# A four-layer transformer kernel: the second layer's feed-forward adapts its weights on VectorE alone, with its even rows spread by a transfer

## The reference, cut to what matters

```python
def _layernorm(x, axis=-1, eps=1e-05):
    m = jnp.mean(x, axis=axis, keepdims=True)
    v = jnp.var(x, axis=axis, keepdims=True)
    return (x - m) / jnp.sqrt(v + eps)

def _L1_ffn_ref(x, W1, b1, W2, b2, scale):          # x: (4, 512, 256), W1: (1024, 256), W2: (256, 1024)
    lt = x[:, 1:17, :]                              # 16 rows of each batch
    even, odd = lt[:, ::2, :], lt[:, 1::2, :]       # 8 rows each
    m1 = (even[:, :4, :, None] * odd[:, :4, None, :]).reshape(4, 1024, 256)
    m2 = (even[:, 4:, :, None] * odd[:, 4:, None, :]).reshape(4, 256, 1024)
    h = einsum('bsd,hd->bsh', x, W1) + scale * einsum('bsd,bhd->bsh', x, m1) + b1
    h = gelu(h)
    return einsum('bsh,oh->bso', h, W2) + scale * einsum('bsh,boh->bso', h, m2) + b2

x = x + _L1_ffn_ref(_layernorm(x), ...)
x = x + _L2_xattn_ref(_layernorm(x), ctx, ...)      # which begins with another layer norm (ln1), times g, plus b
```

## Time and profile before

| | us |
|---|---|
| median of 3 runs | 3356.65 |
| lowest, highest | 3354.74, 3372.45 |
| the profiled execution's own time | 3362.91 |
| its span in the profile | 3361.1 |
| TensorE busy | 2767.6 (82%) |
| VectorE busy | 1979.2 (59%) |
| ScalarE busy | 1440.4 (43%) |
| GpSimd busy | 1143.6 (34%) |
| mean granted clock of TensorE | 0.893 |
| the feed-forward's stage | 941.9 to 1126.3 |

### The profile page before, as it was taken

The page is one execution under the profiler, slowest core; times in us unless marked ns, Lnnn a source line. Parts: engine busy times, 40 slices in busy tenths (PEclk is TensorE's granted clock), DMA queues, the critical chain, the costliest instruction groups (busy, mean ns, idle before and its releaser), DMA issues. The chain is left out here.

```text
span 3361.1 us, 45805 instructions
## 1 busy us (share of the span) xinstructions
PE 2767.6 (82%) x17268; PEld 1590.7 (47%) x17268; DVE 1979.2 (59%) x3643; ACT 1440.4 (43%) x1932; POOL 1143.6 (34%) x1030
## 2 busy tenths in 40 slices
PE   5888887778879899998877898788999998698544
PEld 3343343633336444445743444377777777233122
DVE  4655666577547454445757556664454443677688
ACT  2556556247522254455224455423333432366422
POOL 3233232213133246565325777540010110222333
PEclk7999988889879999999988999889999999699766
DMA  7556651156310001112000000001211121564100
GB/s 170 115 117 142 120 130 34 38 112 136 72 48 1 16 33 40 43 48 72 26 13 1 1 1 1 26 1 37 98 56 43 65 66 51 111 114 105 36 10 15
DMA packets 129740, 198.58 MB, mean 59 GB/s; under 512 B 36272, under 2 KB 66480, under 8 KB 129392
## 3 DMA queue, kind: packets, MB, share of 16 engines
q1 hardware_dynamic: 97776, 143.23, 18.9%
q0 software_dynamic: 31744, 52.41, 5.5%
HBM read 130.73 MB, written 64.75 MB: 58 GB/s over the span
## 5 line engine op out<-in xcount | busy, mean ns | idle before, releaser
L2293 DVE TENSOR_REDUCE L_mx<-bank_t 128x2 f32<-128x1024 f32 (+3 forms) x512 | 565.1, 1121 | 335.0 <-PE bank_t L2104 215.3
L2293 DVE TENSOR_REDUCE L2a_mx<-bank_t 128x2 f32<-128x1024 f32 x256 | 311.4, 1223 | 366.9 <-PE bank_t L2081 366.0
L2500 ACT ACTIVATE L_P<-bank_t 128x1024 f32<-128x1024 f32 (+3 forms) x384 | 340.2, 915 | 255.5 <-PE bank_t L2116 138.9
L2500 ACT ACTIVATE L2a_P<-bank_t 128x1024 f32<-128x1024 f32 x256 | 261.6, 1023 | 285.9 <-PE bank_t L2093 285.6
L2104 PE MATMUL bank_t<-L_KS,L_QS 48*128 48x512 f32 (+2 forms) x1024 | 244.3, 480 | 123.1 <-ACT L_P L2500 47.8
L2081 PE MATMUL bank_t<-L2a_QK 32*128 32x512 f32 x1536 | 251.9, 445 | 75.0 <-ACT L2a_P L2500 30.2
L2116 PE MATMUL bank_t<-L_QS,L_KS 50*128 50x512 f32 (+2 forms) x1024 | 246.4, 485 | 19.0 <-DVE L_mx L2293 9.4
L2089 PE MATMUL bank_t<-L2a_QK 32*128 32x512 f32 x1536 | 256.4, 442 | 0.0
L2081 PEld LDWEIGHTS bank_t<-L2a_QK 32*128 32x128 f32 x1536 | 136.6, 195 | 236.3 <-ACT L2a_P L2500 110.7
L2116 PEld LDWEIGHTS bank_t<-L_QS,L_KS 50*128 50x128 f32 x1024 | 102.0, 199 | 260.9 <-issue 165.5
L2146 PE MATMUL bank_o<-L_P,L_V 128*32 128x512 f32 (+3 forms) x1536 | 204.8, 609 | 8.2 <-ACT L_P L2500 7.0
(11 more groups left out here) (470 smaller groups left out, 6153.5 us busy)
## 6 DMA issues: line engine op xcount, KB each, us to landing
L_KS<-L_spill_k_halves SPq DMA_DIRECT2D x174, 128.0 KB, 5.1
L_QS<-L_spill_q_halves SPq DMA_DIRECT2D x174, 128.0 KB, 4.8
L_spill_raw<-xn POOLq DMA_DIRECT2D x64, 256.0 KB, 2.6
L2g_raw<-in_L_ffn_h_blocks SPq DMA_DIRECT2D x32, 512.0 KB, 3.7
L_spill_k_halves<-L_hi SPq DMA_DIRECT2D x32, 256.0 KB, 2.1
L_spill_k_halves<-L_lo SPq DMA_DIRECT2D x32, 256.0 KB, 2.4
L_spill_q_halves<-L_hi SPq DMA_DIRECT2D x32, 256.0 KB, 2.2
L_spill_q_halves<-L_lo SPq DMA_DIRECT2D x32, 256.0 KB, 2.9
```

The lines of the kernel that those rows point to most:

```text
L2293: e.tensor_reduce(neg, s.tile[:, :, 0:n_keys], AX.X, ALU.max, negate=True).then_inc(sem(s.done), 1)
L2500: e.activation(s.at.Pr[s.pb][:, :, q0:S], s.tile[:, :, q0:S], ACT.Exp, scale=s.at.scale).then_inc(sem(s.exp), 1)
```

## The change

1. The even rows come by transfers. `spread_even(b)` stores the 8 even rows from L1f_lora to DRAM (8x256) and loads them back with the partition dimension broadcast, 128x2048 or 1 MB, into L1f_even. `PickInit` and `PickEven` are gone. SP, which issues both, waits for the first to land before it issues the second.
2. `Adapt` becomes `AdaptOne` (W1e, in the same 8 instructions, but signalled after each 256 columns, so that hidden tile m waits for group m // 2) and `AdaptTwo` (W2e in 32 SCALAR_TENSOR_TENSOR of 128x64). Both run on VectorE alone and are placed by the tables `in_hidden` and `in_output`. `adapt_one(0)` is done in the attention's last unit, into buffers in `keep`.
3. Norms 0 and 1 have their statistics and one root together; norms 2 and 3 are placed by the same tables, norm 3 with the other half of xn.
4. The tail's ticks come one for each hidden tile and two for each output tile of batch 0, and `tail.rest()` behind its output tiles.
5. At the border of attention and feed-forward TensorE is not held any more (L0, L1 and both halves of L2); the banks come free by events instead.
6. The double norm is one: with v the variance of x, the second norm divides by sqrt(v / (v + e) + e), so both together divide by sqrt(v (1 + e) + e * e). `Root` computes that where `twice` is set.
7. Steps of the next attention are put singly and ticked at other places.

```diff
+            even, W1e = [sb(keep, "L1f_even0", [P, 8, C])], [sb(keep, "L1f_W1e0", [P, KC, FF])]
+            odd = [sb(keep, f"L1f_odd{i}", [P, KC, 8]) for i in range(2)]
...
+            def spread_even(b):
+                out_l = landing()
+                add(Store(rows_dram[b], lora[LORA_AT:LORA_AT + 16:2, b, :], [kept[b]], out_l))
+                even_in[b] = load(even[b % 2][:, :, :].rearrange("p j c -> p (j c)"),
+                                  rows_dram[b].rearrange("(a j) c -> a (j c)", a=1).to_broadcast([P, 8 * C]),
+                                  [out_l.done, *even_free[b % 2]])
...
             def steps(st, e_free, ring, busy):
-                turns = lambda b: [lambda k=k: turned(b, k, ring) for k in range(KC)]
-                return [lambda: norm(0), *turns(0), lambda: norm(1), *turns(1)]
+                return [lambda: [statistics(0, 1), roots(0, 1), norm(0), keep_rows(0)],
+                        lambda: [turned(0, 0, ring), spread_even(0)], lambda: turned(0, 1, ring),
+                        lambda: [norm(1), keep_rows(1)], lambda: [adapt_one(0), turned(1, 0, ring)],
+                        lambda: turned(1, 1, ring)]
...
+                in_hidden = {0: {0: [lambda: adapt_two(0)], 3: [lambda: statistics(2)], 4: [lambda: roots(2)],
+                                 5: [lambda: norm(2)], 6: [lambda: adapt_one(1)], 7: [lambda: keep_rows(2)]},
+                             1: {1: [lambda: adapt_one(2)], 3: [lambda: adapt_two(2)], 5: [lambda: statistics(3)],
+                                 6: [lambda: roots(3)], 7: [lambda: norm(3, tail.raw_free)]},
+                             2: {1: [lambda: adapt_one(3)], 3: [lambda: adapt_two(3)]}}
+                in_output = {0: {0: [lambda: adapt_two(1), lambda: turned(2, 0, ring)],
+                                 1: [lambda: turned(2, 1, ring), ready], 2: [lambda: spread_even(2)]},
+                             1: {1: [lambda: keep_rows(3), lambda: turned(3, 0, ring)],
+                                 2: [lambda: turned(3, 1, ring), lambda: spread_even(3)]}}
...
-                    if b == 0:
-                        tail.rest()
                     for t in range(TB):
+                        for step in in_output.get(b, {}).get(t, ()):
+                            step()
+                        if b == 0:
+                            tail.tick()
+                            tail.tick()
...
+                    if b == 0:
+                        tail.rest()
...
+        WRITERS = ("sync", "vector", "scalar", "gpsimd")
...
-                    hold(latest_of_all(), EVERY)
-                ALL.free = [None] * 8
+                    hold(latest_of_all(), WRITERS if follows.own_events else EVERY)
+                ALL.free = tail.bank_free if follows.own_events else [None] * 8
...
+                    if s.twice:
+                        e.tensor_scalar(v, mv[:, s.t0:s.t1, 1], 1.0 + EPS, EPS * EPS, ALU.mult,
+                                        ALU.add).then_inc(step.sem, 1)
...
+                elif kind is AdaptTwo:
+                    dve.wait_ge(*s.after)
+                    for m in range(KF):
+                        r, k = m // KC, m % KC
+                        for i in range(LORA_HALF):
+                            at = slice(i * C // 4, (i + 1) * C // 4)
+                            op = e.scalar_tensor_tensor(
+                                out=s.w2e[:, m, at], in0=s.even[:, 4 + i, :].rearrange("p (q r) -> p q r", r=4)[:, :, r],
+                                scalar=s.odd[:, k, 4 + i:5 + i], in1=s.w2[:, m, at], op0=ALU.mult, op1=ALU.add)
+                    op.then_inc(sem(s.done), 1)
```

More of the change, by code:

```diff
@@ L121 @@
 Keep = namedtuple("Keep", "dst src after done")
-PickEven = namedtuple("PickEven", "pick lora pair bank after mm dst copy_after done")
-Adapt = namedtuple("Adapt", "s w1 w2 w1e w2e even odd odd_cols scale term after w1_done w2_pool w2_vector")
-PickInit = namedtuple("PickInit", "pick done")
+AdaptOne = namedtuple("AdaptOne", "w1 w1e even odd odd_cols scale after odd_done groups")
+AdaptTwo = namedtuple("AdaptTwo", "w2 w2e even odd after done")
 SplitBlock = namedtuple("SplitBlock", "raw row high low after row_after copied free done")
@@ L903, in attention @@
             tail.ot_free, tail.misc = OT_free, misc
+            tail.bank_free = [e for free in tiles.free for e in (free[0], free[0])] + [None, None]
             return tail
@@ new lines, in norm, with keep_rows @@
+            def norm(b, free=()):
+                normal[b] = normalise([(xn[:, slot(b), i, :], X[:, TB * b + i, :], TB * b + i) for i in range(TB)],
+                                      [e_root[b], xn_free[slot(b)], *free])
+            def keep_rows(b):
+                kept[b] = due("lora_kept")
+                add(Keep(lora[:, b, :], xn[0:32, slot(b), 0, :], [normal[b]], kept[b]))
+            def spread_even(b):
[4 more added lines that the diff above has]
+                                  [out_l.done, *even_free[b % 2]])
@@ L1254, in main, with adapt_two @@
                 ring = entry.side.ring = Banks(ALL.aps[:7])
-                e_pick = due("pick_made")
-                add(PickInit(pick, e_pick))
+                ring.free = ALL.free[:7]
+                def adapt_two(b):
+                    i = b % 2
+                    two_done[b] = due("w_two_adapted")
+                    add(AdaptTwo(W2, W2e[i], even[i], odd[i], [even_in[b], odd_done[b], w2_free[i], e_w2_in], two_done[b]))
+                    even_free[i] = [two_done[b], groups[b][-1]]
@@ L1259, in main @@
                 entry.rows()
[L1261 to L1276, removed]
@@ L2174, in tensor_program @@
                     accumulate(s.bank, s.terms).then_inc(sem(s.mm), 1)
-                elif kind is PickEven:
-                    pe.wait_ge(*s.after)
-                    for j in range(2):
-                        mm = e.matmul(s.bank[:, j * C:(j + 1) * C], s.pick[:, 2 * s.pair + j, :], s.lora, start=True,
-                                      stop=True)
-                    mm.then_inc(sem(s.mm), 1)
                 elif kind is Hidden:
```

187 lines of the change are left out of this document (78 added, 109 removed).

## The result

The changed kernel takes 3300.2 us (median of 4 runs, 3299.58 to 3307.12), the one before in the same comparison 3355.69; ratio 0.984, 95% interval 0.9806 to 0.9873. A second comparison gave 0.9818 (0.9792 to 0.9843). The forecast was 3304, in the range 3284 to 3328. The profiled execution has a span of 3305.4 us and took 3307.1.

A forecast was written before the change was run, and what follows sets the result against it. TensorE, busy 82% of the span, was taken to bound the kernel. Stage -45.8, entries -4 and next attention -3 sum to -53 us, 3362.9 to 3310 profiled, so 3304 as median (chance 0.62), range 3284 to 3328.

The forecast's parts named there:

- The picks: TensorE's even-row picks in the changed stage: all 22.5 us go, and the 4.1 us wait for the pick matrix.
- Rival A: Broadcast load of even rows takes 24 us, hidden(0) starts 13 us late: 3322 us; chance 0.12.
- AdaptOne and AdaptTwo: W1e and W2e on VectorE alone in the stage: 4.1 us a set and 8.0 us a batch.
- D: 64-column VectorE instructions cost 0.94 us, AdaptTwo 30 us a batch, VectorE bounds the stage: 3372 us; chance 0.03.
- rival B: VectorE's adapt instructions at upper bounds, 1.0 + 2.9 us a batch, TensorE feels about 12 us: 3316 us; chance 0.13.
- rival C: Credited TensorE waits return under other names, such as banks freed late behind AdaptTwo; three at 5 us: 3319; chance 0.10.
- The walk: Changed stage traced in order: 117.4 us work, 7.0 half clock, 15.5 idle, so 139.9 us instead of 184.4.
- The double norm: VectorE in the stage: three batches save 17 us; not the bound, but TensorE waits for it at three places.
- The attention's end: Attention before the changed stage ends 1.3 us earlier, at 940.6, through shared statistics and root of norms 0 and 1.
- The entries: TensorE no longer held entering the three other feed-forwards: -4 us taken, from 0 to some -8.
- The a1 attention: Next attention, where TensorE waits 9.8 us for maxima: shorter fourth-batch norm gives -3 us, from 0 to -9.8.

The follow-up runs named there:

- five moves: Norm 2 first; then AdaptTwo(1) later; then AdaptTwo(3) too; the second with AdaptTwo(2) behind norm 3; norm 2 first with early bias adds: 3297.2, 3308.4, 3319.5, 3299.6, 3295.7 us.
- norm 2 first: Changed kernel with statistics, root and norm of batch 2 ahead of AdaptTwo(0) in VectorE's queue: 3297.2 us, ratio 0.9823, stage 138.6 us.

## Why the prediction was right

**The picks.** Right, and cheaper than taken: the load landed in 4.4 us (9 was taken, 5 to 24 the bounds), AdaptOne(0) ended at 926.6, 4 us ahead of the attention's end. Rival A fell. The term was 22.5 + 4.1 us; the picks put back cost 17 us of stage, since norm 2 is then ready before hidden(0) ends.

**AdaptOne and AdaptTwo.** 3.26 and 7.63 us where 4.1 and 8.0 were taken; a 64-wide instruction comes every 0.24 us. D fell. The 485 ns that the prediction calls "alone" come from instructions that had begun 0.1 us ahead of POOL's product; the changed kernel, with POOL quiet, has 472 to 486, so the number held. But the sum over a batch held only for those that POOL leaves alone. The prediction took account of the POOL work that the change removes, and not of the bias adds and the product that stay: batch 1's adapts took 16.6 us instead of 10.9. That is more than the 3.9 us a batch of rival B, but in one batch only and by another cause, and the adds to X behind them are rival C's place: 3.9 us of wait where 0.8 was listed.

**The walk.** Stage 143.4 where 139.9 was forecast. TensorE's busy 122.95 against 124.4: half clock cost 5.5 us rather than 7.0, mainly because hidden(0), straight behind the attention, ran at 1.00 and not at 0.50 for its start. Idle 20.4 us against 15.5: norm 2 7.4 (4.3; hidden(0) ended earlier than forecast, the norm ended 20.9 us behind the start as against 20.3), the projection 3.9 (0.8), inner norms 4.8 (5.5), norm 3 none (0.9), gelu 1.6 (2.5), last 2.7 (1.5). The start of hidden(0) at full clock goes with the end of the hold: with TensorE held it starts at the lower one. The double norm was said to matter at these waits without a price for it. Put back by itself into the changed kernel it costs 15 us in the stage, the largest single part beside the picks, and 5 to 6 in the a1 attention of its one profile (455.4; the kernel before, with the double norm in its own order, has 447.1 and 451.0 there). The parts put back one at a time cost 17 us (picks), 15 (double norm) and 9 (W2e shared with POOL). That they add up to the stage's 41 proves little, since waits overlap: 7 us of the picks were hidden by the wait for norm 2.

**Outside the stage.** The attention's end, -1.3: not resolved, as two profiles of each kernel give 286.5 to 292.8 and 284.1 to 287.1. The entries, -4: TensorE's idle of 2.3, 1.4 and 4.5 us at them is gone, and the L0 part is given back; the experiment gives 4 us, which its interval doesn't resolve. The a1 attention, -3: nothing (447.1 and 451.0 against 450.0 and 449.5).

So the mechanism of the stage was right, with -41 us where -44.5 was forecast. That the total came out within 4 us of the forecast is in part luck: everything outside the stage was to give -8, and gave -15 between the two first profiles and -10 between the two second ones, and the two profiles of the kernel before differ by 13 us there. No run here says which part of it the change made.

## What to carry to other kernels

Price a piece of work by what is queued behind it on its engine, not by that engine's busy share: 5.6 us of VectorE ahead of a norm that TensorE waited for cost 5.3 us each time, with VectorE busy for 69% of the stage. When work is moved out of such a queue's way, list first what it is put ahead of; of the five moves here one shortened the stage (norm 2 first, 5 us), and the other four turned one wait into another of about its size or more. And when an engine is taken out of a shared job, look for what it still does at the same time.

## What the runs showed of the hardware

A VectorE instruction with two inputs in SBUF can stand still for the whole of a POOL instruction: 2.45 and 3.02 us instead of 0.35 and 0.48, and not with the POOL adds left out (375 and 486 ns at most). That is what the Trainium skill's page "SBUF — State Buffer" says (Who interferes with whom), and the trace agrees. It costs nothing when VectorE begins first: at the head of each set of the kernel before one took 485 ns with POOL's product running beside it.

Unexpected was that a TENSOR_SCALAR of 128x4 with a single input stood still too (2.80 and 2.20 us instead of 0.17). The same section names tensor_scalar among the operations that can take the shared port pair in a two-port mode, so it does not exclude this. The int32 one between them ran in 0.17 us; it began at 938.68, between POOL's first add and its second. The trace of the kernel before had shown it already, in a norm of the a2 attention:

```profile
2160.75 2.34 POOL L2665 TENSOR_TENSOR L2a_sums<-L2a_sums,L2a_P 128x1024 f32<-128x1024 f32 x1
2161.05 2.06 DVE L2230 TENSOR_SCALAR nw<-mv 128x4 f32<-128x4 f32 x1
```

The fourteen traces have 118 such steps of a root that took 0.9 us or more, 26 of them int32, and each ends within 0.04 us of the end of a POOL tensor instruction.

A 1 MB load that reads 8 KB and writes it to 128 partitions landed in 4.4 us, faster than the plain loads of that size in the same program (6.4 for W1 and W2, 5.2 for L_KT; medians).
